# Requesting x from ScalarE's queue instead of SyncE's

## The chip, the cores and the metric

The kernel runs on one core of one Trainium2 chip. The metric is device time in microseconds (us), the median of several executions. One execution was also taken by the profiler, and all rows below come from it.

## The reference

The input x has 128 samples of 64 channels and 1024 positions. Four layers are added to it one after another; each sees the sum of what came before:

```
x = x + conv1d(x, weight 64x16x9, 4 groups, pad 4) + cond @ c_weight.T + fside
x = x + W1[b] @ x[b] + bias1[b]       # three layers of this kind
x = x + W2[b] @ x[b] + bias2[b]
x = x + W3[b] @ x[b] + bias3[b]
# Wn[b] = sum_k att_n[b,k] * weight_n[k], att_n = softmax(MLP_n(cond[b])), a 64x64 matrix per sample
```

Three 64x64 matrices per sample are multiplied into one, so that each sample sees one grouped convolution and one 64x64 mix. Everything is float32.

## The kernel before, in words

**Work.** The 128 samples are taken in 32 quads of four. Before the quads there is a preamble of some 33 us that computes the per-sample coefficients and two tables of 64x64 matrices. Then there is one step for each quad q:

- x of quad q arrives in `x_sb` (two buffers, `par` = q % 2), one transfer of 128 rows of 8256 bytes, 1032 KB.
- ScalarE rounds it into `x_hi` (`x_high`, L617), VectorE makes the rest `x_lo` (`x_low`, L729). Both are done one step ahead: in step q they are made for q + 1.
- TensorE convolves the four channel groups g = 0..3, six 128x512 matmuls each (`conv`, L406). ScalarE copies each result out of its bank into `conv_sb` (`conv_copy`, L624).
- SyncE moves each group into another layout: `y_sb<-conv_sb` (`move`, L252), 256 KB in rows of 2 KB, four moves per quad. They go from on-chip memory to on-chip memory.
- TensorE mixes (`mix`, L450) the quad before, q - 1, behind the convolution of q. The mix waits for all four moves of q - 1 (`moved`). Behind it TensorE composes matrices (`compose`, L422), which GpSimd has laid out (L347).
- ScalarE and VectorE add the bias while they copy the mixed banks into `out_sb` (`finish`, L631 and L746). SyncE stores `out_sb` of q - 2 (`store`, L245), 1024 KB in rows of 8 KB.

**Order.** Each engine runs its own written list, and semaphores tie them together. The quads from 4 on are in hardware loops of two steps. All the large transfers of a step (one x, four moves, one store) are requested by SyncE, in one queue (q1 in the profile). ScalarE's queue (q10) carries four small transfers at the start, and nothing afterwards.

**The x request.** In step q SyncE requests x of q + 2, into the buffer that x of q has left: it waits until `x_hi` and `x_lo` of q have been made. SyncE comes to this request only after the last move of the step before. ScalarE uses this x in step q + 1.

Of the kernel before, what the change touches and what calls it, by code (L numbers as in the profile page):

```python
# [84 lines left out]
def cond_resid_kernel(nc, x_h, net_h, kept_h, row_h, toep_h, mixrow_h, pairs_h, own_h, out_h):  # L85
    with ExitStack() as ctx:
        def sb(name, shape, dt=F32):
            return ctx.enter_context(nc.sbuf_tensor(name, shape, dt))

        def sem(name):  # L90
            return ctx.enter_context(nc.semaphore(name))
# [68 lines left out]
        x_sb = sb("x_sb", [128, 2, G, S, JX])  # L160
# [27 lines left out]
        x_in = [sem("x_in0"), sem("x_in1")]  # L188
# [12 lines left out]
        xhi_set, xlo_set, conv_done, conv_out = (sem(n) for n in ("xhi_set", "xlo_set", "conv_done", "conv_out"))  # L201
# [27 lines left out]
        def wait(eng, s, value):  # L229

            if not isinstance(value, int) or value > 0:
                eng.wait_ge(s, value)

        block = ctx.enter_context(nc.Block())

        @block.sync
        def _(sp):
            def load(q, par):
                sp.dma_start(x_sb[:, par].rearrange("p g s j -> p (g s j)"),
                             x_h[bass.ds(q * 128, 128), :]).then_inc(x_in[par], 16)  # L240

            def store(q, par):
                sp.wait_ge(out_dve, 2 * q + 2)
                sp.wait_ge(out_act, 2 * q + 2)
                sp.dma_start(out_h[bass.ds(q * 128, 128), :],  # L245
                             out_sb[:, par].rearrange("p s n -> p (s n)")).then_inc(stored[par], 16)

            def move(q, par, g, at):
                if g == 0 and at < 2:
                    wait(sp, mix_done, 2 * TILES * q - 2 * TILES)  # L250
                sp.wait_ge(conv_out, 4 * q + g + 1)
                sp.dma_start(y_sb[g::G, at].rearrange("p h s j -> p h (s j)"),  # L252
                             conv_sb[:, par, g, :]).then_inc(moved[par], 16)

            sp.dma_start(net[:, 0:FIRST], net_h[:, 0:FIRST]).then_inc(net0_in, 16)
            sp.dma_start(net[:, FIRST:], net_h[:, FIRST:]).then_inc(net_in, 16)
            sp.dma_start(row[:], row_h).then_inc(net_in, 16)
            sp.dma_start(pairs, pairs_h).then_inc(pairs_in, 16)
            sp.dma_start(toep_all, toep_h).then_inc(toep_in, 16)
            sp.dma_start(ident[:], kept_h).then_inc(kept_in, 16)  # L260

            n = G // 2 * S * JX
            sp.dma_start(x_sb[:, 0, 0:G // 2].rearrange("p g s j -> p (g s j)"), x_h[0:128, 0:n]).then_inc(x0_first, 16)
            sp.dma_start(x_sb[:, 0, G // 2:].rearrange("p g s j -> p (g s j)"), x_h[0:128, n:]).then_inc(x_in[0], 16)
            sp.dma_start(mixrow, mixrow_h).then_inc(mixrow_in, 16)
            sp.wait_ge(rows21_zero, 1)
            for n in range(2):
                at = OWN + n
                sp.dma_start(mrow[1][at:at + RS * (K - 1) + 1:RS],
                             own_h[K + 1 + K * n:2 * K + 1 + K * n]).then_inc(rows21_in, 16)  # L270
            sp.dma_start(mrow[1][EYE:EYE + 1].rearrange("o (c n) -> o c n", c=16),
                         own_h[3 * K + 1:].rearrange("o (c n) -> o c n", c=16)).then_inc(rows21_in, 16)
            sp.wait_ge(pprod_act, 3)
            sp.wait_ge(pprod_dve, 1)
            for l in range(K):
                sp.dma_start(mrow[1][l:l + RS * (K - 1) + 1:RS].rearrange("m (a n) -> m a n", a=CB),  # L276
                             prod[:, l].rearrange("p c k -> p (c k)")).then_inc(rows21_in, 16)
            sp.wait_ge(toep_lo_set, 1)
            load(1, 1)
            sp.wait_ge(xhi_set, 1)  # L280
            sp.wait_ge(xlo_set, 1)
            load(2, 0)
            for g in range(G):
                move(0, 0, g, 0)

            def step(q, par):
                sp.wait_ge(xhi_set, q + 1)
                sp.wait_ge(xlo_set, q + 1)
                load(q + 2, par)
                move(q, par, 0, par)  # L290
                if not isinstance(q, int) or q >= 2:
                    store(q - 2, par)
                for g in range(1, G):
                    move(q, par, g, par)

            for q in range(1, PEEL):
                step(q, q % 2)
            with sp.Fori(PEEL // 2, NQ // 2 - 1) as it:
                step(2 * it, 0)
                step(2 * it + 1, 1)  # L300
            move(NQ - 2, 0, 0, 0)
            store(NQ - 4, 0)
            for g in range(1, G):
                move(NQ - 2, 0, g, 0)
            for g in range(G):
                move(NQ - 1, 1, g, 2)


            n = 2 * QP * J
            for q in range(NQ - 3, NQ):  # L310
                for p in range(PR):
                    sp.wait_ge(out_act, 2 * q + p + 1)
                    sp.wait_ge(out_dve, 2 * q + p + 1)
                    dst = out_h[q * 128:q * 128 + 128, n * p:n * p + n]
                    if q < NQ - 1:
                        src = out_sb[:, q % 2, 2 * p:2 * p + 2, :].rearrange("p s n -> p (s n)")
                        sp.dma_start(dst, src).then_inc(stored[q % 2], 16)
                    elif p == 0:
                        sp.dma_start(dst, last_out[:, 0:n]).then_inc(stored[1], 16)
                    else:  # L320
                        src = last_out[:, n:2 * n].rearrange("p (s e) -> p s e", s=2)
                        dst = dst.rearrange("p (s e) -> p s e", s=2)
                        for e in range(2):
                            sp.wait_ge(out_act, 2 * q + p + 1 + e)
                            sp.wait_ge(out_dve, 2 * q + p + 1 + e)
                            half = slice(n // 4 * e, n // 4 * e + n // 4)
                            sp.dma_start(dst[:, :, half], src[:, :, half]).then_inc(stored[1], 16)
            sp.wait_ge(stored[0], 16 * (NQ // 2 - 1 + PR))
            sp.wait_ge(stored[1], 16 * (NQ // 2 - 2 + 2 * PR + 1))
# [283 lines left out]
        def _(act):  # L613
            def x_high(q, it, par):
                act.wait_ge(x_in[par], 16 * it + 16)
                wait(act, conv_done, 4 * q - 4)
                nc.scalar.activation(x_hi[:, par].rearrange("p g s j -> p (g s j)"),  # L617
                                     x_sb[:, par].rearrange("p g s j -> p (g s j)"), ACT.Copy).then_inc(xhi_set, 1)

            def conv_copy(q, it, par, g, banks=G):  # L620
                act.wait_ge(conv_done, 4 * q + g + 1)
                if g == 0:
                    wait(act, moved[par], 16 * G * it)
                nc.scalar.activation(conv_sb[:, par, g, :], conv_ps[g % banks][:, :], ACT.Copy).then_inc(conv_out, 1)  # L624

            def finish(q, it, par, p):

                act.wait_ge(mix_done, 2 * TILES * q + TILES * p + TILES)
                if p == 0 and not (isinstance(q, int) and q == NQ - 1):
                    wait(act, stored[par], 16 * it)  # L630
                nc.scalar.activation(result(q, par, 2 * p), pair_banks(q, p)[0][:, :], ACT.Identity,  # L631
                                     bias=beta[:, bass.ds(S * q + 2 * p, 1)]).then_inc(out_act, 1)
# [62 lines left out]
                finish(0, 0, 0, p)  # L695

            def step(q, it, par, it_next, it_prev):
                x_high(q + 1, it_next, 1 - par)
                for g in range(G):
                    conv_copy(q, it, par, g)  # L700
                for p in range(PR):
                    finish(q - 1, it_prev, 1 - par, p)

            step(2, 1, 0, 1, 0)
            step(3, 1, 1, 2, 1)
            with act.Fori(PEEL // 2, NQ // 2 - 1) as it:
                step(2 * it, it, 0, it, it - 1)
                step(2 * it + 1, it, 1, it + 1, it)
# [243 lines left out]
```

## Time and profile before

| | us |
|---|---|
| median of 3 runs | 299.75 (298.91 to 301.86) |
| the profiled execution's own time | 300.04 |
| its span, first to last instruction | 298.2 |
| TensorE busy | 279.2 |
| ScalarE busy | 188.0 |
| VectorE busy | 153.5 |
| GpSimd busy | 97.8 |

The loop takes most of the span: in the window from 66 to 272 us, SyncE requests 25 times x, 100 moves and 25 stores. "Busy" counts instructions only; the share of the DMA engines is a column of its own, and the difference between the time of the execution and its span is start and end outside the instructions.

### The profile page before, as it was taken

How to read it: one execution, taken by the hardware profiler on the slowest of the kernel's cores; microseconds unless marked ns; L12 is line 12 of the kernel's file. 1: busy time of each engine (PE TensorE's matmuls, PEld its weight loads, DVE VectorE, ACT ScalarE, POOL GpSimd, SP SyncE). 2: the span in 40 equal slices, each digit the busy share in tenths (PEclk: the TensorE clock that was granted, in tenths of full speed). 3: DMA queues.
4: the chain of work that ended last, by engine and by line, in shares of the span. 5: the costliest groups of instructions: out<-in, count | busy, mean ns of one | idle time of the engine just before them, and what ended most of it. 6: DMA issues, size and time to landing. Idle time of an engine off the chain costs nothing.

```text
span 298.2 us, 6921 instructions
## 1 busy us (share of the span) xinstructions
PE 279.2 (94%) x1991; PEld 194.2 (65%) x1991; DVE 153.5 (51%) x198; ACT 188.0 (63%) x250; POOL 97.8 (33%) x269
## 2 busy tenths in 40 slices
PE   8898999999899998999999999999999999999982
PEld 7577766666666665666666766666667666666741
DVE  4683864554454445554445544455445545455333
ACT  4665566656567666666667676656667676666642
POOL 2510384441222341444452523411425223414100
PEclk9999999999999999999999999999999999999999
DMA  7869478999999999999999999999999999999887
GB/s 224 238 212 344 166 260 342 377 348 342 349 360 377 361 375 407 381 379 397 386 355 409 387 382 378 383 378 361 369 385 368 375 378 384 376 410 390 333 314 287
DMA packets 30627, 104.55 MB, mean 351 GB/s; under 512 B 3364, under 2 KB 5156, under 8 KB 22921
## 3 DMA queue, kind: packets, MB, share of 16 engines
q1 hardware_dynamic: 30546, 104.29, 93.5%
q10 hardware_dynamic: 72, 0.15, 0.2%
q8 instruction: 5, 0.08, 0.1%
q14 instruction: 4, 0.03, 0.0%
HBM read 36.26 MB, written 33.55 MB: 234 GB/s over the span
## 4 chain that ended last, share of the span: by engine, by line
PE 64%; DMA 24%; SPq 4%; ACT 2%; issue 2%; DVE 1%; ACTq 1%; POOL 0%; DVEq 0%; POOLq 0%
PE bank L406 43%; DMA y_sb<-conv_sb 22%; PE bank L450 15%; PE bank L535 2%; SPq L252 2%; DMA out_sb<-conv_sb 2%; PE bank L422 2%; ACT conv_sb L624 2%; SPq L276 1%; PE bank L506 1%; PE bank L473 1%; ACTq L637 1%; ACT L640 0%; POOL table L333 0%; PE bank L483 0%
## 5 line engine op out<-in xcount | busy, mean ns | idle before, releaser
L347 POOL COPY a<-table 64x64 f32 (+1 forms) x256 | 91.9, 359 | 170.2 <-PE bank L422 118.7
L624 ACT ACTIVATE conv_sb<-bank 128x512 f32<-128x512 f32 x128 | 73.7, 593 | 50.1 <-PE bank L406 49.5
L729 DVE TENSOR_TENSOR x_lo<-x_sb,x_hi 128x2064 fp32r<-128x2064 f32 x31 | 71.6, 2311 | 54.9 <-ACT x_hi L617 51.0
L406 PE MATMUL bank<-x_hi,toep_hi 128*128 128x512 f32 x256 | 84.5, 411 | 0.3 <-DVE x_lo L811 0.3
L746 DVE TENSOR_SCALAR out_sb<-bank,beta 128x512 f32<-128x512 f32 x62 | 46.6, 751 | 70.3 <-PE bank L450 69.6
L406 PE MATMUL bank<-x_hi,toep_lo 128*128 128x512 f32 x256 | 80.9, 398 | 0.0
L406 PE MATMUL bank<-x_lo,toep_hi 128*128 128x512 f32 x256 | 80.8, 397 | 0.0
L450 PE MATMUL bank<-y_sb,mixw 64*64 64x512 f32 (+1 forms) x520 | 62.6, 594 | 9.8 <-DMA y_sb<-conv_sb 8.1
L617 ACT ACTIVATE x_hi<-x_sb 128x2064 fp32r<-128x2064 f32 x31 | 59.7, 1927 | 10.2 <-DMA x_sb<-in_x 10.0
L631 ACT ACTIVATE out_sb<-bank,beta 128x512 f32<-128x512 f32 x62 | 42.6, 688 | 34.9 <-PE bank L450 33.6
L406 PEld LDWEIGHTS bank<-x_lo,toep_hi 128*128 128x128 f32 x256 | 48.3, 189 | 12.0
L406 PEld LDWEIGHTS bank<-x_hi,toep_lo 128*128 128x128 f32 x256 | 48.2, 188 | 11.8
L406 PEld LDWEIGHTS bank<-x_hi,toep_hi 128*128 128x128 f32 x256 | 45.6, 188 | 12.5 <-issue 1.1
L450 PEld LDWEIGHTS bank<-y_sb,mixw 64*64 64x64 f32 x520 | 18.4, 132 | 38.7 <-issue 38.6
L422 PEld LDWEIGHTS bank<-a 64*64 64x64 f32 x512 | 14.6, 134 | 16.3 <-issue 16.3
L739 DVE COPY mixw<-bank 128x128 f32<-128x128 f32 x64 | 15.3, 281 | 1.7 <-PE bank L422 1.7
L422 PE MATMUL bank<-a 64*64 64x64 f32 x512 | 13.8, 218 | 0.0
L535 PEld LDWEIGHTS bank<-coef_t,out_sb 128*128 128x128 f32 x64 | 7.5, 192 | 2.0 <-DMA out_sb<-conv_sb 1.5
L535 PE MATMUL bank<-coef_t,out_sb 128*128 128x128 f32 x64 | 7.8, 277 | 1.1 <-DMA out_sb<-conv_sb 1.1
L800 DVE COPY table<-bank 128x512 f32<-128x512 f32 x8 | 5.3, 684 | 4.3 <-PE bank L535 3.8
L660 ACT ACTIVATE table<-bank 128x512 f32<-128x512 f32 x8 | 4.6, 590 | 2.6 <-PE bank L535 2.6
L457 PE MATMUL bank<-blank 128*128 128x128 f32 x18 | 3.8, 371 | 1.1 <-DVE blank L769 1.1
(74 smaller groups left out, 63.0 us busy)
## 6 DMA issues: line engine op xcount, KB each, us to landing
y_sb<-conv_sb SPq DMA_DIRECT2D x128, 256.0 KB, 6.2
x_sb<-in_x SPq DMA_DIRECT2D x31, 1032.0 KB, 8.3
out<-out_sb SPq DMA_DIRECT2D x29, 1024.0 KB, 8.1
out<-out_sb SPq DMA_DIRECT2D x4, 512.0 KB, 4.1
x_sb<-in_x SPq DMA_DIRECT2D x2, 516.0 KB, 10.2
out_sb<-conv_sb SPq DMA_DIRECT2D x8, 128.0 KB
x_sb<-in_toep SPq DMA_DIRECT2D x1, 640.0 KB, 7.4
out<-x_sb SPq DMA_DIRECT2D x1, 512.0 KB, 3.2
```

The costliest lines, as they stand in the source:

```text
L252: sp.dma_start(y_sb[g::G, at].rearrange("p h s j -> p h (s j)"), conv_sb[:, par, g, :]).then_inc(moved[par], 16)
L347: nc.gpsimd.tensor_copy(dst[rows, par, :, NH * e:NH * e + NH], table[n][C * e:C * e + C, here, h, :]).then_inc(comp_in, 1)
L406: last = mm(o, w[:, d, g, :], v[:, par, g, :, d:d + J], start=i + d == 0, stop=i + d == 3)
L422: last = mm(comp_bank(q, h)[C * r:C * r + C, C * pr:C * pr + C], a21[rows, par, pr, :], a3[rows, par, pr, :], start=True, stop=True)
L450: mm(o, mixw[rows, par, 2 * p + i, :], y_sb[rows, at, m * e:m * e + m, 2 * p + i, :], start=True, stop=True).then_inc(mix_done, 1)
L535: last = mm(bank[BANKS[t]][:, B * i:B * i + B], mrow[1][:, at:at + 2 * C], coef_t[:, 1, :], start=True, stop=True)
L617: nc.scalar.activation(x_hi[:, par].rearrange("p g s j -> p (g s j)"), x_sb[:, par].rearrange("p g s j -> p (g s j)"), ACT.Copy).then_inc( ...
L624: nc.scalar.activation(conv_sb[:, par, g, :], conv_ps[g % banks][:, :], ACT.Copy).then_inc(conv_out, 1)
L631: nc.scalar.activation(result(q, par, 2 * p), pair_banks(q, p)[0][:, :], ACT.Identity, bias=beta[:, bass.ds(S * q + 2 * p, 1)]).then_inc(o ...
L729: nc.vector.tensor_tensor(x_lo[:, par].rearrange("p g s j -> p (g s j)"), x_sb[:, par].rearrange("p g s j -> p (g s j)"), x_hi[:, par].rea ...
L739: nc.vector.tensor_copy(mixw[:, par, h::2, :], comp_bank(q, h)[:, 0:PR * C].rearrange("p (n c) -> p n c", c=C)).then_inc(mixw_set, 1)
L746: nc.vector.tensor_scalar(result(q, par, 2 * p + 1), pair_banks(q, p)[1][:, :], beta[:, bass.ds(S * q + 2 * p + 1, 1)], None, ALU.add).the ...
```

## The change

`load` is now a function outside SyncE's program and takes the engine that issues it. SyncE still requests x of quads 1 to 3. In the steps from quad 2 on, ScalarE requests x of q + 2 as the first thing of its step, behind the same two semaphore waits, and then makes `x_hi` of q + 1. 28 requests (x of quads 4 to 31) change engine and queue. The bytes, rows and buffers are the same.

```diff
+        def load(eng, q, par):
+            eng.dma_start(x_sb[:, par].rearrange("p g s j -> p (g s j)"),
+                          x_h[bass.ds(q * 128, 128), :]).then_inc(x_in[par], 16)
...
             def step(q, par):
-                sp.wait_ge(xhi_set, q + 1)
-                sp.wait_ge(xlo_set, q + 1)
-                load(q + 2, par)
+                if isinstance(q, int) and q < 2:
+                    sp.wait_ge(xhi_set, q + 1)
+                    sp.wait_ge(xlo_set, q + 1)
+                    load(sp, q + 2, par)
                 move(q, par, 0, par)
...
             def step(q, it, par, it_next, it_prev):
+                act.wait_ge(xhi_set, q + 1)
+                act.wait_ge(xlo_set, q + 1)
+                load(nc.scalar, q + 2, par)
                 x_high(q + 1, it_next, 1 - par)
                 for g in range(G):
                     conv_copy(q, it, par, g)
```

The first place is SyncE's loop, its first step. In the kernel before it reads:

```order
L239 ISA [waits xlo_set,xhi_set]
L239 DMA x_sb<-in_x 128x2064
L232 ISA
L251 ISA [waits mix_done]
L252 DMA y_sb<-conv_sb 32x4x512 [waits conv_out]
L243 ISA
L245 ISA [waits out_act,out_dve]
L245 DMA out<-out_sb 128x2048
```

and in the changed kernel:

```order
L251 ISA [waits mix_done]
L252 DMA y_sb<-conv_sb 32x4x512 [waits conv_out]
L243 ISA
L245 ISA [waits out_act,out_dve]
L245 DMA out<-out_sb 128x2048
```

The x request has left; the three other moves, which follow the store, stand as before. The second place is ScalarE's loop, around the border of its two steps, before:

```order
L631 ACTIVATE out_sb<-bank,beta 128x512
L628 REGISTER_ALU
L631 ISA [waits mix_done]
L631 ACTIVATE out_sb<-bank,beta 128x512
L615 ISA
L232 ISA [waits x_in0]
L617 ACTIVATE x_hi<-x_sb 128x2064 [waits conv_done]
```

and in the changed kernel (line numbers are one to four higher there):

```order
L632 ACTIVATE out_sb<-bank,beta 128x512
L629 REGISTER_ALU
L632 ISA [waits mix_done]
L632 ACTIVATE out_sb<-bank,beta 128x512
L237 ISA [waits xlo_set,xhi_set]
L237 DMA x_sb<-in_x 128x2064
L616 ISA
L232 ISA [waits x_in0]
L618 ACTIVATE x_hi<-x_sb 128x2064 [waits conv_done]
```

The request stands behind the last `finish` of the step before and ahead of the rounding of x, for which it now makes ScalarE spend its issue time.

## Rows read from the trace of the kernel before

**Rows 1.** The page's busy time of each engine, share and count.

```profile
PE 279.2 (94%) x1991; PEld 194.2 (65%) x1991; DVE 153.5 (51%) x198; ACT 188.0 (63%) x250; POOL 97.8 (33%) x269
```

**Rows 2.** The page's chain that ended last, by engine.

```profile
PE 64%; DMA 24%; SPq 4%; ACT 2%; issue 2%; DVE 1%; ACTq 1%; POOL 0%; DVEq 0%; POOLq 0%
```

**Rows 3.** Windows: busy time of each engine, then granted clock, DMA share, GB/s.

```profile
66.00:272.00 206.00, 197.60 (x1372) 135.96 (x1374) 104.06 (x124) 135.22 (x174) 70.69 (x200) 1.00 1.00 377
115.00:147.00 32.00, 31.88 (x224) 21.78 (x224) 16.82 (x20) 21.41 (x28) 15.48 (x32) 1.00 1.01 388
180.00:214.00 34.00, 32.17 (x228) 22.25 (x232) 16.82 (x20) 21.95 (x29) 11.55 (x32) 1.00 1.00 373
```

**Rows 4.** DMA view of 66 to 272 us: packets, the queue, requests with time to landing.

```profile
DMA packets 21360, 77.73 MB, mean 377 GB/s; under 512 B 2376, under 2 KB 2376, under 8 KB 15072
...
q1 hardware_dynamic: 21358, 77.71, 99.9%
...
x_sb<-in_x SPq DMA_DIRECT2D x25, 1032.0 KB, 8.3
y_sb<-conv_sb SPq DMA_DIRECT2D x100, 256.0 KB, 6.3
out<-out_sb SPq DMA_DIRECT2D x25, 1024.0 KB, 8.2
```

**Rows 5.** Groups of instructions, 66 to 272 us: busy, mean ns, idle before, releasers.

```profile
L617 ACT ACTIVATE x_hi<-x_sb 128x2064 fp32r<-128x2064 f32 x25 | 48.2, 1928 | 9.3 <-DMA x_sb<-in_x 9.1
L450 PE MATMUL bank<-y_sb,mixw 64*64 64x512 f32 x388 | 47.4, 601 | 8.4 <-DMA y_sb<-conv_sb 8.1
```

**Rows 6.** The chain in order of time (start, us, what), one waiting step.

```profile
238.51 0.60 ACT conv_sb L624
239.11 0.81 SPq L252
...
240.03 7.01 DMA y_sb<-conv_sb
247.03 0.24 issue
247.28 1.95 PE bank L450 x16
```

**Rows 7.** Timeline of SyncE's requests, then of ScalarE, one step: start, us, what.

```profile
125.89 0.35 SPq L239 DMA_DIRECT2D x_sb<-in_x  x1
128.29 0.55 SPq L252 DMA_DIRECT2D y_sb<-conv_sb  x1
129.20 0.35 SPq L245 DMA_DIRECT2D out<-out_sb  x1
129.66 3.70 SPq L252 DMA_DIRECT2D y_sb<-conv_sb  x3
133.72 0.80 SPq L239 DMA_DIRECT2D x_sb<-in_x  x1
...
125.12 0.69 ACT L631 ACTIVATE out_sb<-bank,beta 128x512 f32<-128x512 f32 x1 [0.16 <-PE bank L450]
125.85 1.93 ACT L617 ACTIVATE x_hi<-x_sb 128x2064 fp32r<-128x2064 f32 x1
129.58 0.60 ACT L624 ACTIVATE conv_sb<-bank 128x512 f32<-128x512 f32 x1 [0.81 <-PE bank L406]
130.99 0.60 ACT L624 ACTIVATE conv_sb<-bank 128x512 f32<-128x512 f32 x1 [0.81 <-PE bank L406]
132.37 1.47 ACT L631 ACTIVATE out_sb<-bank,beta 128x512 f32<-128x512 f32 x2 [0.78 <-PE bank L450]
```

**Rows 8.** Issue instructions of the x requests (whole trace) and of moves (100 to 165 us).

```profile
L239 SPq DMA_DIRECT2D x_sb<-in_x x31: 338/487/1011, 18.6 to 267.0; - x31
...
L252 SPq DMA_DIRECT2D y_sb<-conv_sb x32: 536/948/2192, 99.8 to 163.3; - x32
```

**Rows 9.** Landing of the x request of 32.9 us; then moves in 33 to 66 us.

```profile
DMA to landing us min/median/max: 4.8/4.8/4.8
...
y_sb<-conv_sb SPq DMA_DIRECT2D x16, 256.0 KB, 4.7
```

**Rows 10.** Windows near the end: moves alone, then stores alone; columns as in Rows 3.

```profile
281.00:285.00 4.00, 4.00 (x19) 3.20 (x17) 0.00 (x0) 1.79 (x3) 0.00 (x0) 1.00 1.00 391
292.00:295.00 3.00, 1.06 (x20) 0.54 (x12) 1.53 (x3) 1.42 (x3) 0.00 (x0) 1.00 1.02 414
```

More of the change, by code:

```diff
@@ L234, in cond_resid_kernel @@
         block = ctx.enter_context(nc.Block())
+        def load(eng, q, par):
+            eng.dma_start(x_sb[:, par].rearrange("p g s j -> p (g s j)"),
+                          x_h[bass.ds(q * 128, 128), :]).then_inc(x_in[par], 16)
         @block.sync
         def _(sp):
-            def load(q, par):
-                sp.dma_start(x_sb[:, par].rearrange("p g s j -> p (g s j)"),
-                             x_h[bass.ds(q * 128, 128), :]).then_inc(x_in[par], 16)
             def store(q, par):
@@ L278, in _ @@
             sp.wait_ge(toep_lo_set, 1)
-            load(1, 1)
+            load(sp, 1, 1)
             sp.wait_ge(xhi_set, 1)
             sp.wait_ge(xlo_set, 1)
-            load(2, 0)
+            load(sp, 2, 0)
             for g in range(G):
```

## Prediction

> **What bounds the kernel now.** I read the busy times first. TensorE is busy for 279.2 of 298.2 us and no other compute engine for more than 188.0 [rows 1], so it looks like a TensorE kernel with at most a few per cent left. The chain that ended last says otherwise: 24% of it is DMA [rows 2]. So I took the steady loop apart. From 66 to 272 us SyncE makes 25 x requests, so a step lasts 206 / 25 = 8.24 us. The clock is at its full level throughout, and the DMA engines' share is 1.00 at 377 GB/s [rows 3]. TensorE's only large wait there is that of the mix for its moved data, 8.1 us in total [rows 5]. Without it a step would be (206 - 8.1) / 25 = 7.92 us.
>
> The DMA view gives the second bound. A step carries 1032 + 4 x 256 + 1024 KB = 3.15 MB by the request sizes, or 77.71 / 25 = 3.11 MB by the packets counted in the window [rows 4]; at 377 GB/s that is 8.24 us, the length of a step. **Two limits lie 0.32 us apart, and the upper one is the throughput of the DMA engines.** At TensorE's own pace a step asks for more than they deliver, so a queue builds up until the last move of a quad lands too late, TensorE waits, and the queue gets shorter again.
>
> The chain shows where this happens [rows 6]: the last copy of a quad (0.60), its request (0.81), 7.01 us to landing, then the mix. With little in the queue a move lands in 4.7 us, and an x in 4.8 [rows 9]; in the loop x needs 8.3 [rows 4]. The queue that an x request finds ahead of it is thus worth 8.3 - 4.8 = 3.5 us, and the last move can bear 7.0 - 4.7 = 2.3 us of queue before TensorE waits; I call this its **room**.
>
> **The change, part by part.**
>
> *SyncE loses 28 x requests.* They cost it 0.34 to 1.01 us each, median 0.49 [rows 8]. The gap between the end of the last move's request (129.66 + 3.70 = 133.36) and the x request at 133.72 is 0.36 us, and the next move is not asked for until 2.4 us after the x request (125.89 to 128.29) [rows 7], because it waits for ScalarE's copy. SyncE is not what is late; gain 0.
>
> *The time of the request hardly moves.* ScalarE reaches the start of its step when its last `finish` ends, at 125.12 + 0.69 = 125.81, and SyncE's request was at 125.89 [rows 7]. The semaphores it waits for have long been set on both, so the new waits cost nothing.
>
> *ScalarE gains 28 issues.* The rows bound one by 0.34 and 1.01 us, from the same kind of request on SyncE; I take the median 0.49. Today the rounding of x waits for its data for 9.1 / 25 = 0.36 us on average [rows 5]. If x lands earlier this wait goes, so `x_high` moves by about 0.49 - 0.36 = +0.1 us, at most by +1.0. The copies of groups 0 and 1 shift with it, but ScalarE idles for 0.81 us before the copy of group 2 and 0.81 again before that of group 3 [rows 7], the copy that the chain runs through. The cover is 1.6 us; cost on the path 0. If it were gone, each microsecond beyond it would be added to every step.
>
> *The x bytes leave SyncE's order.* This is the only term of size. Today x is requested just behind the last move, so it cannot delay it: it stands behind all of the 3.5 us ahead of it. In its own queue its packets are taken beside those. One x is 1.057 MB, 2.8 us of the engines at 377 GB/s. If both queues are served evenly, x needs 5.6 us, in which SyncE's queue gets through 2.8 of its 3.5 us; the last move, at the end of that queue, comes 2.8 us later. So at the queue depth of today, x lands some microseconds earlier, which nobody needs, and the move that TensorE waits for lands up to 2.8 us later, more than its room. No moves are brought forward by this: of the bytes ahead of a move, those of x are served earlier and not removed.
>
> This can't cost 2.8 us in every step, though. A longer step leaves the engines idle, so the queue gets shorter, and with little queue there is little to overtake. With a depth d at the x request (d under 2.8) and even service, the last move sees d of queue and d of overtaking; 2d = 2.3 gives d = 1.15 us. As long as the queue never runs dry the DMA engines stay busy and the step stays at 8.24 us. The loss is only the time in which they run dry. The queue grows by 0.32 us in a step at TensorE's pace, and the rate itself varies between 373 and 388 GB/s over four steps [rows 3], which is 8.34 against 8.02 us for 3.11 MB. A depth of about 1.15 us mostly covers this. The bounds for this term are 0 and the 2.8 us once in each of 28 steps (78 us, excluded by the argument above); I take 0.3 us of idle engines, one step's growth, in every fifth step: 28 / 5 x 0.3 = 1.7 us.
>
> Sum against the profiled execution: 300.04 + 0 + 0 + 0 + 1.7, about 301.7 us. Its own time is 0.3 us above the median of the runs, so on the median's scale this is 301.5 us.
>
> **The rivals.**
>
> *B, slower: x is served by packets.* The row counts say what packets there are: between 2 and 8 KB 15072 - 2376 = 12696, about 128 for each of 100 moves, so a move consists of 2 KB packets; an x is 128 rows of 8256 bytes, in packets of over 8 KB [rows 4]. If the engines alternate packet by packet, x gets four times the bytes of a move beside it. Then a depth d costs d of queue and 4d of overtaking until x is done: 5d = 2.3, d = 0.46 us. A step's growth of 0.32 us then makes the move up to 5 x 0.32 = 1.6 us late, TensorE waits for that long, and the queue runs dry. Taken as 0.5 us of idle engines in every second to third step this is 0.2 us per step, 28 x 0.2 = 5.6 us: 305.5, and up to 309 at 0.3 us. The store suffers too: requested at 129.20 it lands 8.2 us later, at 137.4, against its next `finish` near 132.37 + 8.0 = 140.4; 3.0 us of room for a delay of 2.8. The point from which B decides is a depth below which the queue can't cover the variations of the rate, about 0.5 us. The Trainium skill says this of the engines, in "DMA: Bandwidth & Descriptors", section "Queues, rings and completion order": each one goes round-robin between the queues that have work, at the granularity of a packet. By that rule alone the time would be B's. No row here has two large queues at work, so I can't confirm it, and its packet may be more than one row's descriptor.
>
> *C, faster: two queues move more bytes.* Stores alone run at 414 GB/s and moves alone at 391 [rows 10], the mixture at 377. If a second queue let it run at 391, a step's 3.11 MB would need 7.95 us, just about TensorE's 7.92; nearly all of the wait goes, 25 x 0.29 = 7 us in the window. The most that can be had is the full 8.1: 292. Half of it gives 296. For it: the mixture is slower than its parts, and the moves' issues take 0.95 us at the median, against a minimum of 0.54 [rows 8], a sign that SyncE's queue is backed up. Against it: the engines' share is already 1.00 [rows 3]. The same page, section "Rules for kernel authors", says that spreading transfers over issuing engines doesn't help bandwidth since they share the 16 DMA engines; with that rule C would be void.
>
> *D, slower: ScalarE gets stuck in the issue.* Some moves' issues last up to 2.19 us [rows 8]. If ScalarE's took that because the transfers of the other queue fill the engines, it would exceed the cover of 1.6 by 0.6 us in every step: 28 x 0.6 = 17 us, 317. The x issues of up to 1.01 us speak against it.
>
> **How the numbers follow.** Less than about 1% can't be told from no change here: 296.8 to 302.7. The forecast, A, has 0.42 and its own range 299 to 304: 0.36 of it within 1%, 0.06 slower. B has 0.26, all slower. C has 0.26: 0.24 faster, 0.02 within 1%. D has 0.06: 0.05 slower, 0.01 within. So faster 0.24, same 0.39, slower 0.37. The range reaches down to C's nearly full gain, 292.5, and up to B at a little over 0.25 us per step, 307.5; left out are the tip of C, B's tail and D.
>
> **What would show it.** In A, the DMA share from 66 to 272 us stays 0.98 to 1.00 and GB/s near 377; x lands 5 to 7 us after its request, the moves' median stays near 6.3, and the mix waits for its move in more steps, for less each. ScalarE no longer waits for x, and still idles before the copies of groups 2 and 3. In B the DMA share falls to 0.95 to 0.97, x lands in under 6 us, and single waits of the mix exceed 1.1 us. In C the GB/s of the same stretch rises to 390 or more and the mix's wait shrinks. In D the idle time before ScalarE's copies of groups 2 and 3 is gone. The forecast is wrong if the rate of the DMA engines with two queues differs from 377 by more than 1%, either way: nothing in this trace measures it.

## The result and the profile after

The changed kernel takes 327.35 us (322.68 to 329.42), against 300.29 for the kernel before in the same sessions: a ratio of 1.080 with an interval of 1.067 to 1.093. It is 8% slower. The forecast of 301.5 us was wrong, and so was its range up to 307.5; slower by over 1% had been given 0.37. The profiled execution took 329.4 us, with a span of 327.5. Medians here are over all runs and ratios over the runs within 1.5% of the fastest of their kernel, so that the ratio is 1.080 where 327.35 / 300.29 would give 1.090, and the profiled run is the slowest of its four, at the same mean granted clock (0.962, the others 0.957 to 0.967).

The page first: busy time, the queues, and the chain by engine and by line, cut.

```profile
PE 289.2 (88%) x1991; PEld 197.0 (60%) x1991; DVE 153.7 (47%) x198; ACT 187.8 (57%) x250; POOL 102.0 (31%) x269
...
q1 hardware_dynamic: 26514, 74.70, 58.9%
q10 hardware_dynamic: 4104, 29.74, 26.8%
...
PE 56%; DMA 31%; SPq 5%; ACT 3%; issue 2%; DVE 1%; ACTq 0%; POOL 0%; DVEq 0%; POOLq 0%
```

Against [rows 1, 2], the other engines do the same work, and TensorE is idle for 327.5 - 289.2 = 38.3 us instead of 19.0. That is 19.3 us of the 29.3 by which the span grew. The other 10.0 us are TensorE's own busy time, 289.2 against 279.2 for the same 1991 matmuls (a matmul takes longer when the granted clock is low).

The windows of the changed kernel show both (columns as in [rows 3]): the loop, then one wait of the mix, what followed it, and three microseconds more.

```profile
66.00:298.00 232.00, 205.72 (x1366) 138.09 (x1364) 104.00 (x123) 135.71 (x173) 72.84 (x199) 0.96 0.90 338
182.00:187.00 5.00, 0.95 (x8) 0.46 (x7) 0.27 (x1) 0.76 (x2) 0.36 (x1) 0.95 0.96 368
187.00:190.00 3.00, 3.00 (x16) 1.12 (x20) 0.71 (x1) 0.69 (x1) 0.00 (x0) 0.51 0.70 278
190.00:193.00 3.00, 3.00 (x31) 2.28 (x24) 1.19 (x4) 2.01 (x2) 1.24 (x6) 1.00 0.32 75
```

TensorE stands still for four of the five microseconds from 182 to 187. Then its granted clock is 0.51, the lower of its two levels (1.2 of 2.4 GHz), and a few microseconds later the DMA engines run dry: 75 GB/s from 190 to 193, because new moves need TensorE's results, and it had stood still. Over the loop the DMA share is 0.90 and a step takes 206 / 22 = 9.36 us (88 moves from 66 to 272 us), against 8.24.

The chain of that place, in order of time, to be read beside [rows 6]:

```profile
175.01 0.60 ACT conv_sb L625
175.62 1.17 SPq L252
...
176.90 9.95 DMA y_sb<-conv_sb
186.84 0.14 issue
186.98 3.39 PE bank L451 x16
190.37 0.23 PE bank L423 x16
```

A DMA piece of the chain is counted from the start of the instruction that requests it. The last move takes 9.95 us to land where the chain of before had 7.01, and the mix behind it 3.39 us instead of 1.95. Of the eight waits of this kind between 100 and 300 us, six have 9.1 to 10.0 us and two 7.0 to 7.4; in the kernel before all are 7.0 to 7.4.

When was x requested? The issue instructions of this move and of this x (ns, start in us):

```profile
L252 SPq DMA_DIRECT2D y_sb<-conv_sb x1: 1247/1247/1247, 176.9 to 176.9; - x1
L237 ACTq DMA_DIRECT2D x_sb<-in_x x1: 339/339/339, 177.3 to 177.3; - x1
```

SyncE takes 1.25 us to request the last move, until 178.14, and ScalarE asks for x in the middle of it, at 177.33. At the six late moves x was requested 0.4 to 1.4 us after the start of the last move's request, which is between 0.8 us before its end and 0.7 us behind it. In the kernel before, from 100 to 272 us, x always came behind that end, by 0.36 or 0.68 us.

The DMA view of two single microseconds, 180 to 181 and 181 to 182 us, shows who was served (packets, MB, share):

```profile
q10 hardware_dynamic: 31, 0.26, 82.2%
q1 hardware_dynamic: 15, 0.02, 6.4%
```

```profile
q10 hardware_dynamic: 37, 0.30, 119.0%
q1 hardware_dynamic: 6, 0.01, 3.1%
```

The last move has been pending in SyncE's queue (q1) all this time. x, in ScalarE's (q10), moves 0.56 of the 0.59 MB. The lead doesn't last. Over 179 to 186 us, nearly all of x's service, it is about even by bytes:

```profile
q10 hardware_dynamic: 140, 1.03, 53.2%
q1 hardware_dynamic: 410, 1.17, 41.9%
```

**x overtakes: all of its 1.06 MB is served before the last move has landed, part of it in a burst in which SyncE's queue gets next to nothing.** x lands at 186.5, the last move at 186.85. The medians hide this: the moves' landing fell from 6.3 to 5.3 us (66 to 272 us), as the waits leave many of them an empty queue; their longest is 9.9.

One more thing stands in [rows 6] that the prediction passed over. The copy of the last group ended at 239.11, and SyncE began the last move's request only at 240.03. In between it was busy with the third move. The issue instructions of the third and the last move there, in the kernel before:

```profile
L252 SPq DMA_DIRECT2D y_sb<-conv_sb x1: 1554/1554/1554, 238.4 to 238.4; - x1
L252 SPq DMA_DIRECT2D y_sb<-conv_sb x1: 1203/1203/1203, 240.0 to 240.0; - x1
```

The 0.81 us of SPq in that chain are the tail of the third move's request, and the last move's own request takes another 1.20 us, inside the 7.01. **SyncE is late for the last move, in both kernels.** In the changed one it began 1.3 us after the copy in the chain above.

### The profile page after: what moved, and what is told of

Its sections match the earlier page's. It is cut to its first block, busy times and chain, and to the rows that moved or that the text cites. A ratio compares the mean times of both kernels' runs of the same rounds, so it can differ in the third digit from the quotient of the medians.

```text
span 327.5 us, 6921 instructions
## 1 busy us (share of the span) xinstructions
PE 289.2 (88%) x1991; PEld 197.0 (60%) x1991; DVE 153.7 (47%) x198; ACT 187.8 (57%) x250; POOL 102.0 (31%) x269
## 4 chain that ended last, share of the span: by engine, by line
PE 56%; DMA 31%; SPq 5%; ACT 3%; issue 2%; DVE 1%; ACTq 0%; POOL 0%; DVEq 0%; POOLq 0%
PE bank L407 36%; DMA y_sb<-conv_sb 30%; PE bank L451 14%; SPq L252 3%; PE bank L536 2%; ACT conv_sb L625 2%; PE bank L423 2%; DMA out_sb<-conv_sb 2%; SPq L276 1%; PE bank L507 1%; ACTq L638 0%; ACT L641 0%; PE bank L474 0%; POOL table L334 0%; PE bank L484 0%
## 5 line engine op out<-in xcount | busy, mean ns | idle before, releaser
L348 POOL COPY a<-table 64x64 f32 (+1 forms) x256 | 96.2, 376 | 197.8 <-PE bank L423 147.1
L451 PE MATMUL bank<-y_sb,mixw 64*64 64x512 f32 (+1 forms) x520 | 71.1, 665 | 30.0 <-DMA y_sb<-conv_sb 28.5
L407 PE MATMUL bank<-x_hi,toep_hi 128*128 128x512 f32 x256 | 85.5, 416 | 0.3 <-DVE x_lo L815 0.3
L451 PEld LDWEIGHTS bank<-y_sb,mixw 64*64 64x64 f32 x520 | 19.5, 145 | 62.2 <-issue 62.1
L423 PEld LDWEIGHTS bank<-a 64*64 64x64 f32 x512 | 15.3, 142 | 19.7 <-issue 19.7
```

Of the source, the lines that this page charges most:

```text
L348: nc.gpsimd.tensor_copy(dst[rows, par, :, NH * e:NH * e + NH], table[n][C * e:C * e + C, here, h, :]).then_inc(comp_in, 1)
L407: last = mm(o, w[:, d, g, :], v[:, par, g, :, d:d + J], start=i + d == 0, stop=i + d == 3)
L423: last = mm(comp_bank(q, h)[C * r:C * r + C, C * pr:C * pr + C], a21[rows, par, pr, :], a3[rows, par, pr, :], start=True, stop=True)
L451: mm(o, mixw[rows, par, 2 * p + i, :], y_sb[rows, at, m * e:m * e + m, 2 * p + i, :], start=True, stop=True).then_inc(mix_done, 1)
```

## The experiments

Three theories were set against each other: overtaking (O), a lower rate of the DMA engines with x read from a second queue (R), and the issue on ScalarE itself (I). Times are medians; ratios are to runs of the kernel before on the same chip.

**e3, a small transfer in x's place.** x stays on SyncE.

```diff
...
             def step(q, it, par, it_next, it_prev):
+                wait(act, tiny_in, 16 * (q - 2))
+                nc.scalar.dma_start(tiny[:], x_h[bass.ds(q * 128, 16), 0:128]).then_inc(tiny_in, 16)
                 x_high(q + 1, it_next, 1 - par)
```

> The kernel before, where ScalarE also issues one transfer of 8 KB (16 rows of 512 bytes of x into an unused tile) at the very place where the changed kernel requests x; x stays on SyncE's queue. 28 issues of 0.34 us and nearly no bytes. I: most of the loss shows, 310 us or more. O and R: 300 us, within 2 us, since the issue is covered by ScalarE's idle time.

Measured: 302.44 us, ratio 1.001 (0.995 to 1.006). I is out: 28 issues on ScalarE, of 8 KB each, and a second queue in use cost nothing that the interval would show.

**e4, x ahead of the last move in one queue.** The diff shows the step; the first and last steps are fitted to it.

```diff
-                load(q + 2, par)
                 move(q, par, 0, par)
                 if not isinstance(q, int) or q >= 2:
                     store(q - 2, par)
-                for g in range(1, G):
+                for g in range(1, G - 1):
                     move(q, par, g, par)
+                sp.wait_ge(xhi_set, q + 2)
+                sp.wait_ge(xlo_set, q + 2)
+                load(q + 3, 1 - par)
+                move(q, par, G - 1, par)
...
```

> The kernel before, all in SyncE's one queue, but x of the quad after next is requested just ahead of the last move and not just behind it (its buffer is free by then). So x overtakes the last move in one queue. O: the last move has 2.8 us more ahead of it, more than its 2.3 us of room, and the time goes up as in the changed kernel: 312 to 330 us. R and I: there is no second queue, the rate is that of before, and the time stays at 298 to 304 us.

Measured: 338.0 us (331.6 to 344.6) against 301.0, 12% slower and 8 us beyond the range that O gave. Its loop has the marks of the changed kernel, without a second queue:

```profile
66.00:272.00 206.00, 176.76 (x1168) 116.97 (x1167) 86.07 (x105) 113.76 (x146) 80.26 (x168) 0.93 0.89 319
```

So 1 MB ahead of the last move is enough for the whole effect. In its chain the last move needs 7.6 to 9.7 us from its request to its landing.

**e1 and e2, the store behind the last move**, in the kernel before and in the changed one.

```diff
                 move(q, par, 0, par)
-                if not isinstance(q, int) or q >= 2:
-                    store(q - 2, par)
                 for g in range(1, G):
                     move(q, par, g, par)
+                if not isinstance(q, int) or q >= 2:
+                    store(q - 2, par)
```

> The kernel before with one line moved: SyncE requests the store of a step behind the last move and not behind the first, so that 1.05 MB (2.8 us at 377 GB/s) no longer stand ahead of the last move. Three theories stand for the 27 us that the change cost. O (overtaking): the bytes of x, in their own queue, are served ahead of the last move, which then lands later than TensorE can bear, and in the wait the DMA engines run dry. R (rate): with x in a second queue the DMA engines deliver less while x is read. I (issue): a transfer on ScalarE's queue is itself the trouble. This is the control for the next run. O: the last move has more room, the step is still bound by the throughput of the engines, 8.24 us or slightly less if the rate allows; 295 to 300 us. R and I: the same, since neither ScalarE's queue nor the order of x is touched. Over 303 us would say that the late store holds up the copies into out_sb.

> The changed kernel with the same move of the store behind the last move. O: the store's 2.8 us are no longer ahead of the last move, which pays for the 2.8 us of x that overtake it; the waits of the mix nearly vanish and the time falls to 298 to 304 us. R: the engines still deliver less while x is read from its own queue, so at least half of the loss stays: 312 us or more. I: nothing changes on ScalarE's queue, 320 us or more.

Measured: e1 306.6 us, ratio 1.010 (1.004 to 1.016); e2 306.1 us, ratio 1.005 (0.998 to 1.012). The control lies above O's 295 to 300, because the wait moves on: ScalarE now waits 50 us for x and 30 us for stores, while the moves land in 3.5 us. e2 lies 2 us above O's range. With x on ScalarE's queue this order costs nothing more than with x on SyncE's. That direction is O's; R wanted 312 us or more, I 320, and both are contradicted.

**e5 and e6, stores cut to 64 KB**, before and changed. Most of the output is left unwritten.

```diff
-                sp.dma_start(out_h[bass.ds(q * 128, 128), :],
-                             out_sb[:, par].rearrange("p s n -> p (s n)")).then_inc(stored[par], 16)
+                sp.dma_start(out_h[bass.ds(q * 128, 128), 0:128],
+                             out_sb[:, par, 0, 0:128]).then_inc(stored[par], 16)
```

> The kernel before, with each store of the loop cut to 64 KB (128 rows of 512 bytes; most of the output of these quads stays unwritten). A step then asks for about 2.2 MB, 5.8 us of the DMA engines, far under TensorE's 7.92. Control for the next run. Overtaking and rate agree: no queue, no waits of the mix, TensorE's pace, 287 to 293 us.

> The changed kernel with the same cut. Overtaking: it needs a queue to jump. With 5.8 us of transfers in a step the engines are done before the next x is requested, so the two kernels take the same time within 1%. Rate (the engines deliver less while x comes from its own queue) or a fixed cost of the second queue: the x reads are as slow as before the cut and still meet the moves, the kernel stays 2% or more above the control.

Measured: 290.7 and 289.6 us. The two are within 0.4%, at TensorE's pace, with x and moves landing in 4.8 and 2.4 us in both. Without a queue to jump, the change is free.

**e7, x as four transfers with rows of 2 KB**, on ScalarE's queue. `x_high` then waits for all four, which the diff leaves out.

```diff
...
+                for g in range(G):
+                    eng.dma_start(x_sb[:, par, g].rearrange("p s j -> p (s j)"),
+                                  x_h[bass.ds(q * 128, 128), S * JX * g:S * JX * (g + 1)]
+                                  ).then_inc(x_in[par] if g == G - 1 else x_more[par], 16)
...
```

> The changed kernel, but ScalarE requests x as four transfers of one group each, rows of 2 KB and not of 8 KB; same bytes, same place, three more issues of 0.34 us (covered: 1.36 of 1.6 us). If the engines alternate between the queues row by row, x has 80% of them beside a move today and would have 50% now, so the last moves are delayed less: 305 to 318 us. If they share by bytes or by larger units: 320 to 330 us as in the changed kernel. If it is overtaking as such, whatever the share (x always ends before the end of SyncE's queue), then also 320 to 330 us.

Measured: 322.05 us, ratio 1.068 (1.058 to 1.078), little better than the change, and in the range for a share that doesn't go by rows (320 to 330). It says less than it should: 13% of its chain is ScalarE's issue of these transfers, and `x_hi` waits up to 3.9 us for it. Issues on ScalarE can block after all, when four follow each other. The share by rows stays untested.

**e8, the store on ScalarE's queue, x on SyncE's.** SyncE's program loses it.

```diff
...
                 x_high(q + 1, it_next, 1 - par)
-                for g in range(G):
+                conv_copy(q, it, par, 0)
+                act.wait_ge(out_dve, 2 * q - 2)
+                act.wait_ge(out_act, 2 * q - 2)
+                nc.scalar.dma_start(out_h[bass.ds(q * 128 - 256, 128), :],
+                                    out_sb[:, par].rearrange("p s n -> p (s n)")).then_inc(stored[par], 16)
+                for g in range(1, G):
                     conv_copy(q, it, par, g)
```

> The kernel before, where the store of a step goes to ScalarE's queue (issued behind the copy of group 0, as early as now) and x stays on SyncE's. Now the second queue holds bytes that already stood ahead of the last move, so nothing overtakes it that was not ahead of it before. Overtaking: moves land at the same time or earlier, the step stays at the throughput of the engines, 297 to 303 us; faster only if two queues raise the rate above 377 GB/s. Rate or the second queue itself: 1 MB a step in a second queue costs as in the changed kernel, 312 us or more.

Measured: 291.95 us, ratio 0.970 (0.963 to 0.977), faster than O's 297 to 303, and far from R's 312 or more. ScalarE issues this store while it still rounds x, ahead of the first move.

**e9, the control for it: one queue, the store ahead of the first move.**

```diff
-                move(q, par, 0, par)
                 if not isinstance(q, int) or q >= 2:
                     store(q - 2, par)
-                for g in range(1, G):
+                for g in range(G):
                     move(q, par, g, par)
```

> The kernel before, all in SyncE's one queue, with the store requested ahead of the first move and not behind it. Control for the store on ScalarE's queue (292 us): there the store also starts some 1.5 us earlier. If the gain came from the earlier request, this kernel shows it too: 291 to 296 us. If it came from the second queue (moves and stores side by side, 390 instead of 377 GB/s), this one stays at 298 to 304 us, bound by the same rate as the kernel before. Overtaking: the last move has the same bytes ahead of it as before, no loss.

Measured: 290.75 us, ratio 0.963 (0.955 to 0.972), the fastest of all. The second queue was not needed. Its loop, and the issue instructions of its moves:

```profile
66.00:272.00 206.00, 203.70 (x1420) 139.33 (x1420) 107.41 (x126) 139.84 (x179) 99.71 (x205) 1.00 1.01 389
```

```profile
L252 SPq DMA_DIRECT2D y_sb<-conv_sb x103: 529/552/1394, 67.6 to 271.3; - x103
```

The same bytes in the same queue move at 389 GB/s with a share of 1.01, where the kernel before had 377 with 1.00 [rows 3]. So 377 was no capacity.

What moved is SyncE. In a step of this kernel whose mix waits, the chain has no request of another move between the copy and the last move, and the last move's own request takes 0.53 us instead of 1.20:

```profile
239.40 0.61 ACT conv_sb L623
240.00 0.02 issue
240.02 8.02 DMA y_sb<-conv_sb
```

```profile
L252 SPq DMA_DIRECT2D y_sb<-conv_sb x1: 529/529/529, 240.0 to 240.0; - x1
```

At the median of quads 6 to 28, the request of the last move began 1.1 us after the copy in the kernel before and took 1.24; here 0.02 and 0.53. So it is made 1.8 us sooner after the copy, and the mix's wait falls from 8.1 to 2.0 us. That the sooner request is what gives the 3.7%, and not some other effect of the order, is the likely reading; no run isolates it.

**e10, the store on ScalarE's queue, x ahead of the last move** (the edits of e4 and e8 together).

> The store on ScalarE's queue, as in the 292 us kernel, and x requested just ahead of the last move in SyncE's queue, as in the kernel that took 338 us. Overtaking: what x ahead of the last move costs depends on the room that is left. The moves no longer stand behind a whole store, so part of the 2.8 us is affordable: 300 to 325 us, clearly over 292 and clearly under 338. If the loss of the 338 us kernel was only that the mixture ran slowly in one queue, this one stays at 292 to 297.

Measured: 329.4 us, ratio 1.096 (1.086 to 1.107). x ahead of the last move costs as much as in e4, 37 us above the kernel without that order in both cases (e8, on another chip, and the kernel before). O's expectation, that the smaller queue would make part of it affordable (up to 325), was not met.

**e11, x and store on ScalarE's queue** (the change with the edit of e8).

> The changed kernel with the store on ScalarE's queue too, behind x, so that SyncE's queue holds nothing but the moves. Overtaking: x still comes beside the last move, but the store is no longer ahead of the moves in their queue; at the time of the x request the moves' queue is short, they get half of the engines and land in 5 us or less. Time 290 to 300 us. Rate of reads in the second queue as the cause: the slow stretches of the changed kernel stay, 310 us or more.

Measured: 339.6 us, ratio 1.126 (1.110 to 1.141). O (290 to 300) missed it by far; R's 310 or more is met. The moves have a queue to themselves, and a last move needs 10.9 us. One microsecond in its flight, 186 to 187 us:

```profile
q10 hardware_dynamic: 47, 0.33, 88.8%
q1 hardware_dynamic: 1, 0.00, 0.5%
```

A queue with few small transfers is not favoured beside one that holds 2 MB; in this microsecond it gets one packet of 48. So the mechanism of O, bytes of another queue served ahead of the last move, is at work, and its premise that the moves would get half of the engines is wrong.

**e12, x requested behind the rounding of the x before.**

```diff
+                x_high(q + 1, it_next, 1 - par)
+                act.wait_ge(xhi_set, q + 2)
                 act.wait_ge(xlo_set, q + 1)
                 load(nc.scalar, q + 2, par)
-                x_high(q + 1, it_next, 1 - par)
```

> The changed kernel, still with x on ScalarE's queue, but ScalarE asks for it behind the rounding of the x before (it waits for that to be done), some 2.2 us later in the step. By then more of the last move's queue has been served. Overtaking: 2.2 us less of x beside the last move, so most of the loss goes: 300 to 315 us. Rate or queue: x is read from the same queue in the same size, no gain: 320 us or more.

Measured: 356.15 us, ratio 1.178. A bad experiment: the new wait closes a loop, in which x lands (8.4 us), is rounded (1.9), and only then is the next x asked for. Its chain shows it:

```profile
144.13 8.36 DMA x_sb<-in_x
...
152.61 1.94 ACT x_hi L618
154.70 8.43 DMA x_sb<-in_x
```

Its time fits R's 320 or more and not O's 300 to 315, but with the loop closed it tells nothing about either.

**e13 and e14, the last move on ScalarE's queue**, in the changed kernel and in the one before. SyncE's program loses it.

```diff
...
                 for g in range(G):
                     conv_copy(q, it, par, g)
+                act.wait_ge(conv_out, 4 * q + 4)
+                act.wait_ge(mix_done, 2 * TILES * q - 2 * TILES)
+                nc.scalar.dma_start(y_sb[G - 1::G, par].rearrange("p h s j -> p h (s j)"),
+                                    conv_sb[:, par, G - 1, :]).then_inc(moved[par], 16)
```

> The changed kernel, but ScalarE also requests the last move of each quad itself, right behind its copy and so ahead of the next x in the same queue. x can no longer overtake the last move, only the second and third, which are needed no earlier than it. Overtaking with the second queue served first: the last move lands early and the time falls to 290 to 305 us. Reads from a second queue as the cause (they lower the rate): x is where it was, 315 us or more.

> Control for the run above: the kernel before with the last move of each quad on ScalarE's queue, x on SyncE's. Overtaking: the last move jumps the store and the other moves, which are then the late ones, by 0.7 us less than the last one was; nothing of x is ahead of them. 290 to 302 us. If a second queue as such costs, 310 us or more.

Measured: e14 296.4 us, ratio 0.987 (0.981 to 0.993); e13 323.3 us, ratio 1.075 (1.065 to 1.085), a miss for O as I had put it. The chain shows what is late instead, the third move on SyncE's queue, whose request began at 165.07 and took 1.21 us, with x requested at 166.96, 0.7 us behind its end:

```profile
165.07 10.71 DMA y_sb<-conv_sb
```

Protecting one move of four is not enough; the mix needs all of them. By its time alone e13 would fit R, so one more was needed.

**e15, the change with the store ahead of the first move** (the edit of e9).

> The changed kernel, with the store requested ahead of the first move as in the kernel of 291 us. Overtaking: the order before the last move does not change what overtakes it. It starts with less queue, so part of the loss may go, but x still comes beside the last moves: 305 to 330 us. If the change was slow only because moves and store were badly ordered, 291 to 296 us.

Measured: 302.1 us against 300.6, below O's 305 to 330 and above the 291 to 296 of a mere bad order. Its four runs lie at 296 to 298 and at 307, and only one of the first two was profiled. The loop of that run, 297.6 us:

```profile
66.00:272.00 206.00, 201.99 (x1406) 136.48 (x1407) 106.50 (x129) 136.73 (x176) 60.88 (x203) 0.99 1.01 386
```

x is on ScalarE's queue here and the engines move 386 GB/s: **R is out**, as reads of x from a second queue don't lower the rate by themselves. In its chain a late move, of 8.6 and 9.3 us, comes twice in the whole loop. SyncE is on time here as in e9, and the last move lands before x in every step from 66 to 272 us. Against e9 (290.75, on another chip) the x request on ScalarE still costs some 11 us at the median, 6 for the two faster runs.

**What the theories are worth.** R is contradicted by e2, e4, e8 and e15; only e11 and e13 fit it by their times, and e12, which tests nothing. O has the direction of e2, e4, e6 and e10, and the late moves in the traces of e4, e10, e11 and e13. As a way to foresee times it was poor: e1, e2, e4, e8, e10, e11, e13 and e15 all lie outside its ranges. And e15 has the same x request on the same queue as the changed kernel at a fraction of its loss. The second queue alone is therefore not the whole cause. What sets e15 apart is the store's place and, with it, a SyncE that is on time.

## Why the prediction was wrong, point by point

**What bounds the kernel: half right.** The wait of the mix for the last move is where everything happens. That the upper limit was "the throughput of the DMA engines" at 377 GB/s was wrong: e9 and e8 move the same bytes at 389 and 390. A DMA share of 1.00 meant that transfers were always under way, not that no more could be moved.

**ScalarE's issues: right.** e3 shows them to be free, and each took 0.34 us.

**SyncE and the time of the request: wrong.** That the lost requests gain SyncE nothing may stand. But "SyncE is not what is late" doesn't: the prediction took the 0.81 us in [rows 6] for the last move's request, where they are the third's. It also had x still "just behind" the last move. And it let ScalarE come to the x request when its last `finish` ends. The request is issued before that end, here by 176.32 + 1.47 - 177.33 = 0.46 us:

```profile
176.32 1.47 ACT L632 ACTIVATE out_sb<-bank,beta 128x512 f32<-128x512 f32 x2 [0.71 <-PE bank L451]
177.33 0.34 ACTq L237 DMA_DIRECT2D x_sb<-in_x  x1
```

So x passes a SyncE that is still busy with the last move.

**The x bytes leave SyncE's order: the mechanism right, its consequence wrong.** "The move that TensorE waits for lands up to 2.8 us later" is what happened: 9.95 against 7.01 us. The step that failed is the one behind it: "This can't cost 2.8 us in every step", with a queue that settles at a depth of 1.15 us by even service and runs dry for 0.3 us in every fifth step, 1.7 us in all. The runs show two things in its place.

- The queue doesn't settle. It swings between a late move and an empty queue, since TensorE, whose results the next moves carry, stands still for up to four microseconds at a time. The DMA share over the loop is 0.90, so the engines lack work for 10% of it, and a step takes 9.36 us and not 8.24.
- The sum had no term for TensorE's clock: after such a wait it falls to 0.51, and the same matmuls take 10.0 us longer in all.

That service would be even is not far off over the whole of an x (1.03 against 1.17 MB), though not within it. The 4.7 us for a move "with little in the queue" was too much: with the stores cut a move lands in 2.4 us (e5), so the room is 4.6 us and not 2.3. That error would make the loss smaller, not larger.

**Rival B named the right side and place, at a fifth of the size.** It had x favoured, a dry queue every second to third step and single waits over 1.1 us; the waits and the dry queue are in the trace, the large ones every second to sixth step. x favoured by four to one is there only in bursts, and x landed in 7.7 us at the median, not in the under 6 that B gave as its sign. Its 0.2 us per step measured 9.36 - 8.24 = 1.1 us. (Its upper end of 309 is 308 by its own 0.3 us in each of 28 steps.) The rule of the Trainium skill behind it ("DMA: Bandwidth & Descriptors", section "Queues, rings and completion order": round-robin between queues, packet by packet) agrees with the direction. B took one row of 8 KB as the packet; the records show longer runs of one queue, 37 of x against 6 in a microsecond, and 47 against 1 in e11. By the Trainium skill, in the same section, a packet is typically 9 to 17 descriptors. An x is 128 rows over 16 engines, 8 rows for each, so by that figure a turn could be a whole x, an estimate that such bursts fit and that no run here tests.

**Rival C** (two queues move more) is void for x. The rate did rise to 390 with the store in the second queue, but e9 gets 389 from one. This agrees with the Trainium skill, the same page's "Rules for kernel authors", which expects no bandwidth from spreading transfers over issuing engines. **Rival D** did not happen for one transfer in a step; e7 shows that it can for four.

**What stays open.** What decides whether x gets ahead of the last move. Counted from the end of the last move's request, x comes at -0.8 to +0.7 us at the late moves of the changed kernel and mostly at +1.0 to +1.5 in e15, where it rarely overtakes. But the two late moves of e15 have +0.8 and +1.2, and other steps of the changed kernel have -0.02 to +0.7 and no wait of over 1.4 us; in five of these eight the queue had just been empty (the first move of the quad landed in 1.9 to 2.1 us, against 4.3 to 5.4 at the late ones). So distance and depth both seem to count, and no run varies either alone. How much of the 10.0 us of clock would remain without the waits was not tried either.

## What to carry to other kernels

Keeping a bulk request behind the last urgent transfer in one queue was worth 8% here: a queue that is always full is also an order of priority, and a second queue gives it up. Check first whether the engine that issues the urgent transfer gets to it in time. Here SyncE came about 1 us late, which let the other engine's request pass, and in a chain the time of an issue instruction may belong to the transfer before. Where transfers and the engine that produces them wait for each other, price a delay by what stops with it, the next transfers and TensorE's clock, and not by the idle time of a steady flow. And before calling a DMA share of 1.00 a limit, try another order of the same requests: moving one store ahead of the first move gave 3.7%.

## What the runs showed of the hardware

- With two queues pending, one can take nearly everything for a microsecond or two: 0.30 of 0.31 MB in one microsecond of the changed kernel, 47 of 48 packets in one of e11. Over the seven microseconds around the first it was 1.03 MB against 1.17.
- A share of 1.00 to 1.01 went with 377, 386, 389 and 390 GB/s for the same transfers in different orders and queues.
- Issuing a 256 KB transfer took SyncE between 0.54 and 2.37 us in the loop of the kernel before. The two requests nearest to the store's took 0.54 to 0.67 us in the step of [rows 6], the third and fourth 1.55 and 1.20; with the store behind the last move (e1) the median of all was 0.54. On ScalarE one 1032 KB request took 0.34 us, and of four 258 KB requests in a row each took 0.65 at the median and up to 1.58.
- After TensorE had stood still for some four microseconds, its granted clock was 0.51 in the next three, and the matmuls of a mix took 3.4 us instead of 1.95.
